# Expert MLP of a graph block: three slots instead of two for the split second weight matrix, and the last chunk's copy ahead of its GELUs

## What is computed

```python
h = layernorm(x) * ln_g + ln_b                       # 1250 tokens, 512 wide
vals, idx = top_k(h @ w_r.T + b_r, 2)                # 8 experts, two per token
gates = softmax(vals)
hid = gelu(h @ W1[e] + b1[e])                        # 512 -> 2048
y = hid @ W2[e] + b2[e]                              # 2048 -> 512
x = x + sum(gates * y over the token's two experts)
```

## Time and profile before

| | |
|---|---|
| median of three runs | 2231.49 us (2231.03 to 2235.07) |
| the profiled execution | 2244.3 us |
| its span (first to last instruction) | 2242.7 us |
| busy: PE, DVE, ACT, POOL | 2060.6, 1310.2, 1055.9, 642.1 us |
| the expert stage | 940 to 1572 us of the span, 23 tiles |

### The profile page before, as it was taken

One profiled execution on the slowest core, in us unless ns is written; L12 is line 12 of the kernel. 1 busy time (PEld: TensorE's weight loads), 2 busy tenths in 40 slices (PEclk: granted clock), 3 DMA queues, 4 the chain that ended last, 5 costly groups with the idle time before them and its releaser, 6 DMA issues.

```text
span 2242.7 us, 45115 instructions
## 1 busy us (share of the span) xinstructions
PE 2060.6 (92%) x13564; PEld 1490.1 (66%) x13565; DVE 1310.2 (58%) x2831; ACT 1055.9 (47%) x2327; POOL 642.1 (29%) x759
## 2 busy tenths in 40 slices
PE   7899888888888988799999999999599999989998
PEld 4444344444444438588888888888388888778886
DVE  3212788888888876655555555555712356454444
ACT  6531333333333323276777777767143232464443
POOL 3102678787777774300000000002200000210000
PEclk9999999999999998699999999999899999989999
DMA  6642577767677678455603420042700200220000
GB/s 218 219 165 90 154 191 194 189 188 188 187 190 192 188 213 313 154 204 194 242 19 121 157 77 19 19 168 64 279 16 10 85 20 19 76 75 10 10 10 18
DMA packets 157292, 288.53 MB, mean 129 GB/s; under 512 B 43533, under 2 KB 85270, under 8 KB 152615
## 3 DMA queue, kind: packets, MB, share of 16 engines
q1 hardware_dynamic: 111349, 158.80, 20.5%
q0 software_dynamic: 37552, 121.91, 19.0%
q10 hardware_dynamic: 8322, 6.89, 0.9%
HBM read 233.69 MB, written 53.85 MB: 128 GB/s over the span
## 4 chain that ended last, share of the span: by engine, by line
PE 60%; DVE 18%; issue 10%; ACT 3%; DMA 3%; DVEq 2%; POOL 2%; POOLq 0%; another core or an unknown queue 0%; ACTq 0%; SPq 0%
PE psum L2583 14%; PE psum L2722 6%; DVE big_b L1747 5%; PE psum L2755 4%; DVE big_b L1748 4%; PE psum L2628 4%; PE psum L2573 4%; PE psum L2574 3%; PE psum L2575 3%; PE psum L2619 3%; PE psum L2659 3%; PE psum L2649 3%; DVE wide L1738 2%; DVE big_b L1746 2%; PE psum L2301 2%
## 5 line engine op out<-in xcount | busy, mean ns | idle before, releaser
L1049 POOL DMA_INDIRECT big_b<-sender_table,wide x360 | 366.9, 1019 | 94.9 <-issue 91.9
L1260 ACT ACTIVATE wide<-wide 128x290 bf16<-128x290 f32 x360 | 169.4, 528 | 283.7 <-remote 196.0
L2432 PEld LDWEIGHTS psum<-big_b,wide 128*32 128x32 f32 x3600 | 166.3, 109 | 194.6 <-issue 135.2
L2583 PEld LDWEIGHTS psum<-xn_T,big_b 128*128 128x128 f32 x2048 | 261.9, 191 | 21.2 <-issue 3.1
L2402 PE MATMUL psum<-w_mlp,wide 64*128 64x512 f32 x728 | 206.8, 645 | 73.1 <-issue 44.4
L2432 PE MATMUL psum<-big_b,wide 128*32 128x256 f32 (+2 forms) x3600 | 272.2, 390 | 0.0
L2583 PE MATMUL psum<-xn_T,big_b 128*128 128x128 f32 x2048 | 265.0, 275 | 0.0
L1924 DVE TENSOR_TENSOR w_lo<-wide,w_hi 128x512 fp32r<-128x512 f32 x184 | 127.3, 692 | 118.0 <-ACT w_hi L1360 118.0
L2573 PE MATMUL psum<-w_hi,hid_hi 128*128 128x512 f32 x368 | 175.8, 478 | 12.9 <-DVE w_lo L1924 7.2
L1748 DVE TENSOR_TENSOR big_b<-big_b,psum 128x768 f32<-128x768 f32 x180 | 170.1, 945 | 0.0
L1747 DVE TENSOR_TENSOR big_b<-big_b,psum 128x768 f32<-128x768 f32 x180 | 169.6, 942 | 0.0
(11 more groups left out here) (460 smaller groups left out, 3862.5 us busy)
## 6 DMA issues: line engine op xcount, KB each, us to landing
big_a<-in_L_ffn_W SPq DMA_DIRECT2D x12, 2048.0 KB, 11.4
big_b<-in_L_ffn_W SPq DMA_DIRECT2D x12, 2048.0 KB, 13.7
wide<-in_L_ffn_W SPq DMA_DIRECT2D x8, 2048.0 KB, 23.4
wide<-edge_hidden SPq DMA_DIRECT2D x182, 64.0 KB
edge_hidden<-wide SPq DMA_DIRECT2D x21, 512.0 KB, 3.0
tokens_sorted<-zeros SPq DMA_DIRECT2D x29, 256.0 KB
adj_dram<-big_a SPq DMA_DIRECT2D x1, 6400.0 KB, 23.1
xn_T<-tokens_sorted POOLq DMA_DIRECT2D x25, 256.0 KB, 2.9
```

Of the source, the lines that this page charges most:

```text
L1049: nc.gpsimd.indirect_dma_start(out=sent[q][:, j, :], out_offset=None, in_=sender_table, in_offset=bass.IndirectOffsetOnAxis(ap=indices[j], ...
L1260: last = nc.scalar.activation(hot_step[q][:, j, :, :], block_steps[k], ACT.Sign, bias=record[q][:, j, Y + 1:Y + 2])
L2432: nc.tensor.matmul(msg_psum[k].rearrange("p (c u) -> p c u", u=MUL)[bands[g], cols, :], hot_y[q][:, j, y, :], p[:, of, :], start=False, st ...
L2583: last = nc.tensor.matmul(psum[:, f % UP_BANKS, 0:P], ew1[a][:, c, f * P:f * P + P], tile_T[:, c, :], start=(c == 0), stop=(c == C - 1))
```

## The change

The two parts of a chunk of W2 go into rings of three slots. Slots 0 and 1 are those of before; the third ones are laid into the free space of xn_T, whose rows are otherwise laid out as before. The copy of chunk f waits for the last reader of slot f % 3: that is down(f - 3) for f of 3 and more, and in the tile before down(15) for chunk 0, down(13) for chunk 1 and down(14) for chunk 2. On ACT the copy of chunk 15 now stands ahead of the GELUs of chunk 15, and on DVE the rest of chunk 15 ahead of hidden_rest(15).

```diff
+            overlay.enter_context(nc.sbuf_tensor("hid_full", [P, HID_SLOTS * P], F32R))
+            w2_hi_third = overlay.enter_context(nc.sbuf_tensor("w2_hi_third", [P, D], F32R))
+            overlay.enter_context(nc.sbuf_tensor("tile_and_gates", [P, C * NP - 5 * D], F32R))
+            w2_lo_third = overlay.enter_context(nc.sbuf_tensor("w2_lo_third", [P, D], F32R))
...
+        W2_SLOTS = 3
+        w2_hi_slot = [w2_hi[:, 0, :], w2_hi[:, 1, :], w2_hi_third[:, :]]
+        w2_lo_slot = [w2_lo[:, 0, :], w2_lo[:, 1, :], w2_lo_third[:, :]]
...
             def w2_leading(t, a, f):
-                act.wait_ge(chunk_used, t * FC + f + HID_SLOTS - 1)
-                nc.scalar.activation(w2_hi[:, f % 2, :], w2_chunk(a, f), ACT.Copy).then_inc(w2_hi_ready, 1)
+                slot_used_by = f - W2_SLOTS if f >= W2_SLOTS else -1 - (FC - 1 - f) % W2_SLOTS
+                act.wait_ge(chunk_used, t * FC + slot_used_by + 1 + HID_SLOTS)
+                nc.scalar.activation(w2_hi_slot[f % W2_SLOTS], w2_chunk(a, f), ACT.Copy).then_inc(w2_hi_ready, 1)
...
-                            if f + 1 < FC - 1:
+                            if f + 1 < FC:
                                 w2_leading(t, a, f + 1)
-                            if f == FC - 1:
-                                w2_leading(t, a, f)
...
-                nc.vector.tensor_tensor(w2_lo[:, f % 2, :], w2, w2_hi[:, f % 2, :].bitcast(F32), ALU.subtract).then_inc(w2_split, 1)
+                nc.vector.tensor_tensor(w2_lo_slot[f % W2_SLOTS], w2, w2_hi_slot[f % W2_SLOTS].bitcast(F32), ALU.subtract)\
+                    .then_inc(w2_split, 1)
...
                             hidden_rest(t, f)
-                            if f + 1 < FC - 1:
+                            if f + 1 < FC:
                                 w2_rest(t, a, f + 1)
-                        w2_rest(t, a, FC - 1)
                         tile_transposed_out(t + 2)
...
-                            h, w = f % HID_SLOTS, f % 2
+                            h, w = f % HID_SLOTS, f % W2_SLOTS
...
+                            nc.tensor.matmul(psum[:, Y_BANK, :], hid_hi[:, h, :], w2_hi_slot[w], start=(f == 0), stop=False)
+                            nc.tensor.matmul(psum[:, Y_BANK, :], hid_lo[:, h, :], w2_hi_slot[w], start=False, stop=False)
+                            nc.tensor.matmul(psum[:, Y_BANK, :], hid_hi[:, h, :], w2_lo_slot[w], start=False, stop=(f == FC - 1))\
```

More of the change, by code:

```diff
@@ L2570, in down @@
                             pe.wait_ge(hid_split, t * FC + f + 1)
-                            h, w = f % HID_SLOTS, f % 2
-                            nc.tensor.matmul(psum[:, Y_BANK, :], hid_hi[:, h, :], w2_hi[:, w, :], start=(f == 0), stop=False)
-                            nc.tensor.matmul(psum[:, Y_BANK, :], hid_lo[:, h, :], w2_hi[:, w, :], start=False, stop=False)
-                            nc.tensor.matmul(psum[:, Y_BANK, :], hid_hi[:, h, :], w2_lo[:, w, :], start=False, stop=(f == FC - 1))\
+                            h, w = f % HID_SLOTS, f % W2_SLOTS
+                            nc.tensor.matmul(psum[:, Y_BANK, :], hid_hi[:, h, :], w2_hi_slot[w], start=(f == 0), stop=False)
+                            nc.tensor.matmul(psum[:, Y_BANK, :], hid_lo[:, h, :], w2_hi_slot[w], start=False, stop=False)
+                            nc.tensor.matmul(psum[:, Y_BANK, :], hid_hi[:, h, :], w2_lo_slot[w], start=False, stop=(f == FC - 1))\
                                 .then_inc(chunk_used, 1)
```

## The result

The changed kernel takes 2219.28 us (median of six, 2215.65 to 2222.15) where the kernel before, run beside it, takes 2233.89 us (2231.03 to 2235.36). The ratio is 0.9936, with a 95% interval of 0.9923 to 0.9949: 14.3 us faster, between 11.4 and 17.2. The forecast was 10.2 us, and the range reached from 3 to 14 us: 2219.28 us lies inside the range of 2217.3 to 2228.7 us, and the distance of 14.3 us, taken against the runs beside it, lies at its far edge. The profiled execution took 2219.92 us with a span of 2218.3 us. That is 24.4 us less than the span before, more than the medians differ; 8.5 us of it lie ahead of the first up product of the stage (939.81 before, 931.30 after), in code that the change does not touch.

The account below looks back on a forecast made before the run. PE bounds the kernel (busy 92%), waiting for w2_lo at each tile's end. 20 x 0.58 = 11.6 us gained less 3 x 0.47 = 1.4 lost gives 10.2 us, from 2231.49 to 2221.3 us; range 2217.3 to 2228.7.

Parts of the forecast that it names:

- The end of a tile: Down(15) follows down(14) at once, its first weight load hidden: about 0.58 us gained per tile, lower end 0.48.
- rival 1: At down(15) the first weight load stays exposed: 7.9 us gained, 2223.6 us; chance 0.15.
- What is late next: Before down(15), hid_lo(15) is ready 0.31 us early; before up(0), the turned tile about 0.4 us early.
- Rival 2: Down(15) waits for hid_lo(15), or up(0) for the turned tile: 4.4 us gained, 2227.1 us; chance 0.09.
- The new wait on chunk 0: Next tile's chunk 0 copy needs down(15): covered by 0.9 us, except three even-expert boundaries losing 0.47 us each.
- a load stands behind the wait of its ACTIVATE: At three even-expert boundaries ACT's table load starts 0.43 us after down(15)'s last matmul, 0.47 us later than before.
- The starts of a turn: Where a turn of i opens, the longer wait is met during loop-bound loading; gain 0.58 us as in other tiles.
- The clock: At starts of turns of i two clock falls stay, about 1.7 us each; none would give 3.3 us more.
- Rival 3: Clock falls at even-expert boundaries where PE waits 2.0 us: 2233.2 us; chance 0.04, one or two falls 0.12.
- The third slot itself: In mid-tile chunks the third slot gains nothing; PE stays at 1.58 us per chunk.
- Rival 4: The change does not act, PE being held at a tile's end by its own loop: 2231.5 us; chance 0.04.

Follow-up runs that it names:

- third kernel: The changed kernel with DVE's old order alone (rest of chunk 15 behind hidden_rest(15) again); ratio 0.9954 to the kernel before.
- fourth kernel: The changed kernel with ACT's chunk 0 wait in an instruction of its own ahead of the copy; ratio 0.9936 to the kernel before.

## Why the prediction was right, and where its sizes were off

- *The end of a tile*, 0.58 us: right to the hundredth, 26.44 to 25.86 us. Down(15) follows after 0.24 us; the weight load hides, and rival 1 fell. With it fell, for this shape, the sentence of the Trainium skill (TensorE: Matmul & The Clock Gate, The mechanism) that a weight load overlaps matmuls in flight only where the row group differs: these matmuls share all rows, and the load of 1094.21 still runs beside the matmul of 1094.20. The same section of the Trainium skill also names loads into a background weight buffer as ones that are pulled ahead. The prediction left that out; the overlap seen here agrees with it, though no row shows the buffer.
- *What is late next*: hid_lo(15) is ready at 1093.84, 0.36 us ahead of the last matmul of down(14); 0.31 was forecast. DVE's half of the turned tile is ready at 1094.67 and ACT's at 1094.75 (1093.94 + 0.81), 0.40 us ahead of up(0). Rival 2 fell, and the third kernel shows how near it was: DVE's old order has w_lo(15) ready 0.24 us behind that matmul, and down(15) is 0.06 us late.
- *The new wait on chunk 0*: covered in the odd tiles, as forecast. In the three second tiles of even experts the term was wrong in sign: a loss of 0.47 us each was forecast, and a gain of 0.19 us each was measured. The step that failed is "a load stands behind the wait of its ACTIVATE". Here the load started 0.16 us before the last matmul of down(15), for which the copy had to wait, and not 0.43 us behind it. PE's wait for hid_lo grew by 0.39 us and not by 1.05. I had the rule from L1384, which waits for two semaphores where the copy waits for one. Why the load stood behind the wait there, I take to be that two waits need an instruction of their own ahead of the load; no trace shows that. The fourth kernel shows the part that matters: with a waiting instruction of its own ahead of the copy, the load is released by down(15) and each of these tiles is 0.65 us longer.
- *The starts of a turn*: taken as 0.58 us each like other tiles, they gave 0.81 to 0.91 in the start of up(0). The sum had no term for the loop bounds at all: up(0) of a turn came forward by more than the matmuls ahead of it did (0.57 us), but by less than PE's last wait (1.00 us).
- *The clock*: I kept two falls; they became one, and shorter, in each profile of the changed kernel. I had put a change of the clock into the range and not into the sum, and with its cause open, that it went the good way is luck as far as the forecast goes. Rival 3, more falls where PE waits longer, did not come: PE's wait for hid_lo(0) is 1.11 us there, not the 2.0 us on which that rival rested, and no fall follows. The fourth kernel has 1.76 us, and none follows there either.
- *The third slot itself*: chunks stay 1.59 us apart (1090.93 to 1092.52 in the trace after; the mean over all mid-tile chunks is 1.587 us before and after): nothing, as taken. Rival 4 fell with the gain.

The sum again: 10.2 forecast, plus 3 x (0.47 + 0.19) = 2.0 for the even tiles, plus 3 x 0.29 = 0.9 for the bounds, plus 2.7 for the clock makes 15.8 us. That is what the stage showed from the end of the first tile on; the medians say 14.3 (11.4 to 17.2). The direction and the mechanism of a tile's end were right. The forecast lay below the measured interval because all three sizes that were off erred to the same side. The three added terms were read off the same trace that they explain, so that the sum agrees is bookkeeping and no test.

## What to carry to other kernels

Here the deeper ring paid only because the copy that it frees was also issued early: look for the one place per tile where the order of an engine's program, and not the slot, holds the copy, and move both together. When the producer's lead is exposed once per tile, price it from the starts of matmuls, not from modelled idle time, and count what follows the wait (a hidden weight load, and at a loop's start whatever else hangs on that wait) into the gain. Before adding a wait ahead of a function table load, look whether it rides on the ACTIVATE or stands in front of the load.

## What the runs showed that I had not expected

- The function table load ran ahead of the one wait of its ACTIVATE (959.68, with the last matmul of down(15) still to start at 959.84), and behind a wait that stood as an instruction of its own (0.65 us per tile in the fourth kernel).
- Arriving 0.06 us late for a stream of matmuls costs 0.17 us (26.03 instead of 25.86 us per tile), since the first weight load is exposed too.
- At the top of a turn of i, up(0) comes 3.7 to 3.9 us after PE's last wait, 2.4 to 2.9 us of it idle. With the turns written out and the bounds loaded ahead that idle time is gone from the turns, some 1.7 us stand once ahead of the stage, and four table loads are left of fourteen.
